# A graph network and mixture of experts on one core: attention's node blocks in thirteen pieces instead of ten

## Time and profile before

| | us |
|---|---|
| median of 3 runs | 1982.28 |
| lowest and highest | 1980.02, 2367.55 |
| the profiled execution | 1982.39 |
| its span, first to last instruction | 1980.4 |
| TensorE busy | 1654.1 (84%) |
| VectorE busy | 964.8 (49%) |
| GpSimd busy | 793.4 (40%) |
| ScalarE busy | 574.2 (29%) |
| mean granted clock of TensorE | 0.903 |

### The profile page before, as it was taken

How to read it: one execution, slowest core, us unless ns; L and a number is a source line. 1 busy time by engine, 2 the same in 40 slices (tenths; PEclk the granted TensorE clock), 3 DMA queues, 4 the chain that set the end, 5 groups by cost and what they waited for, 6 DMA issues and landing times.

```text
span 1980.4 us, 22491 instructions
## 1 busy us (share of the span) xinstructions
PE 1654.1 (84%) x6593; PEld 1039.0 (52%) x6593; DVE 964.8 (49%) x2223; ACT 574.2 (29%) x1334; POOL 793.4 (40%) x769
## 2 busy tenths in 40 slices
PE   5899575987979969997256889999899989989886
PEld 2454122444544545554133566667676766766665
DVE  5522141223333333434377677776676677764222
ACT  2121000212213223231022344343434344442321
POOL 1000565577656656000367545444445454420000
PEclk9899666998999989998667899999998999999888
DMA  7256454455445455201679755545545454421000
GB/s 244 112 181 217 132 137 134 114 158 147 129 143 160 130 172 133 85 17 59 190 226 281 227 146 151 148 138 159 151 132 159 141 167 139 143 84 33 19 6 8
DMA packets 191723, 269.97 MB, mean 136 GB/s; under 512 B 28484, under 2 KB 156193, under 8 KB 189025
## 3 DMA queue, kind: packets, MB, share of 16 engines
q1 hardware_dynamic: 147585, 144.74, 23.4%
q0 software_dynamic: 44000, 123.64, 22.5%
HBM read 196.22 MB, written 72.06 MB: 135 GB/s over the span
## 4 chain that ended last, share of the span: by engine, by line
PE 34%; DVE 6%; issue 4%; ACT 3%; SPq 1%; DMA 1%; POOL 1%; another core or an unknown queue 0%; POOLq 0%; ACTq 0%; DVEq 0%
PE att_psR L2262 8%; PE att_psR L2289 7%; PE att_psG L2147 5%; PE att_psR L2237 4%; PE att_psR L2246 4%; PE att_psQ L2123 1%; PE att_psR L2223 1%; PE att_psE L2130 1%; DVE att_stat L1911 1%; PE att_psR L2195 1%; POOL att_kv L1769 1%; PE att_psR L2200 1%; PE att_psR L2281 1%; DVE att_n L1922 1%; PE att_psG L2146 1%
## 5 line engine op out<-in xcount | busy, mean ns | idle before, releaser
L1769 POOL DMA_INDIRECT att_kv<-table_kv,g_srcI x314 | 357.9, 1140 | 502.7 <-PE att_psG L2147 274.5
L1085 POOL DMA_INDIRECT ex_hg<-table_h,z_idx x314 | 312.2, 994 | 185.5 <-issue 88.6
L1382 PE MATMUL ex_psG<-ex_hg,ex_oh 128*42 128x256 f32 x628 | 182.5, 433 | 59.0 <-issue 23.3
L2262 PE MATMUL att_psR<-att_t,g_mw 128*128 128x256 f32 x640 | 183.6, 438 | 18.6 <-ACT att_t L2101 18.6
L2147 PE MATMUL att_psG<-att_kv,att_oh 128*42 128x264 f32 x628 | 171.2, 414 | 1.8 <-issue 1.0
L2262 PEld LDWEIGHTS att_psR<-att_t,g_mw 128*128 128x128 f32 x640 | 135.7, 219 | 48.8 <-issue 28.2
L1382 PEld LDWEIGHTS ex_psG<-ex_hg,ex_oh 128*42 128x42 f32 x628 | 72.7, 130 | 168.8 <-issue 92.6
L1789 DVE TENSOR_TENSOR att_kv<-att_kv,att_epb 128x1024 f32<-128x1024 f32 x79 | 96.4, 1221 | 115.4 <-ACT att_epb L2058 97.2
L719 PE MATMUL tab_psH<-e_u,tab_xT 128*128 128x512 f32 x320 | 145.4, 607 | 7.2 <-DVE e_u L521 7.2
L2289 PE MATMUL att_psR<-g_mw,att_h 128*128 128x256 f32 x640 | 149.9, 382 | 0.0
L2289 PEld LDWEIGHTS att_psR<-g_mw,att_h 128*128 128x128 f32 x640 | 122.4, 192 | 20.4 <-issue 3.3
(11 more groups left out here) (308 smaller groups left out, 2443.4 us busy)
## 6 DMA issues: line engine op xcount, KB each, us to landing
table_h<-tab_hs SPq DMA_DIRECT2D x20, 1024.0 KB, 3.9
att_eft<-in_eft SPq DMA_DIRECT2D x158, 64.0 KB
ex_db<-table_dst SPq DMA_DIRECT2D x79, 126.0 KB
table_ohT<-ex_ohT SPq DMA_DIRECT2D x79, 126.0 KB
att_ohT<-table_ohT SPq DMA_DIRECT2D x79, 126.0 KB
table_oh<-ex_oh SPq DMA_DIRECT2D x79, 84.0 KB
att_oh<-table_oh SPq DMA_DIRECT2D x79, 84.0 KB
table_x<-e_x SPq DMA_DIRECT2D x10, 512.0 KB, 4.7
```

The costliest lines, as they stand in the source:

```text
L1085: nc.gpsimd.indirect_dma_start(hg[:, t % RING0, :], None, d.h[:, :], bass.IndirectOffsetOnAxis(ap=g.idx0[:, t:t + 1], axis=0)).then_inc(go ...
L1382: ins = nc.tensor.matmul(psG[0:WG, 0:D], oh[:, i % 3, t % TP, :], hg[:, t % RING0, :], start=(t % TP == 0), stop=last)
L1769: nc.gpsimd.indirect_dma_start(kv[:, t % (RINGC * TP), H:H + 2 * D], None, d.kv[:, :], bass.IndirectOffsetOnAxis(ap=g.srcI[:, t:t + 1], ax ...
L2262: ins = nc.tensor.matmul(out[:, c * CB:(c + 1) * CB], g.mw1[:, e, k, c * P:(c + 1) * P], t3[:, k, :], start=(k == 0), stop=(k == DK - 1))
```

## The change

`SEGMENTS` has thirteen pieces; `turnA` gets an own piece behind `att`, `turnN` and `turnX` too, and the first products `f` and `A` stand a slot behind their turn. `att` is now VectorE's part alone. In a slot where pieces of two blocks meet, `mix` stands behind `A` 2. The last block starts at slot 87 instead of 89. The banks: outside `f` to `norm` units turn over three; from the first `f` to `norm` they alternate on two (0 and 1) while `y` holds bank 2. The bursts of zero products are gone.

```diff
-WARM = 12
...
 SEGMENTS = (
     (("att", 0),),
+    (("turnA", 0),),
     (("wo", 0),),
-    (("turnN", 0), ("f", 0), ("f", 1), ("y", 0), ("f", 2), ("y", 1)),
-    (("f", 3), ("y", 2), ("f", 4), ("y", 3), ("f", 5), ("y", 4)),
-    (("f", 6), ("y", 5), ("f", 7), ("y", 6), ("y", 7), ("norm", 0)),
-    (("turnX", 0), ("A", 0), ("logits", 0), ("A", 1)),
-    (("mix", 0), ("A", 2), ("C", 0), ("A", 3)),
+    (("turnN", 0),),
+    (("f", 0), ("f", 1), ("y", 0), ("f", 2), ("y", 1), ("f", 3), ("y", 2)),
+    (("f", 4), ("y", 3), ("f", 5), ("y", 4), ("f", 6), ("y", 5)),
+    (("f", 7), ("y", 6), ("y", 7), ("norm", 0)),
+    (("turnX", 0),),
+    (("A", 0), ("logits", 0), ("A", 1)),
+    (("A", 2), ("mix", 0), ("C", 0), ("A", 3)),
     (("C", 1), ("A", 4), ("C", 2)),
     (("A", 5), ("C", 3), ("A", 6), ("C", 4)),
     (("A", 7), ("C", 5), ("C", 6), ("C", 7), ("out", 0)))
...
-    start = [(NG // NC + 1) * (b + 1) + LAG + 2 if slots else 8 * b + 1 for b in range(NC)]
+    start = [min((NG // NC + 1) * (b + 1) + LAG + 2, SLOTS + 1) if slots else 8 * b + 1 for b in range(NC)]
...
-        bank, before, last, turn_of = {}, {}, {}, 0
+        bank, before, last, turn_of, opened = {}, {}, {}, 0, False
         for what, b, e in order:
-            for unit in {"att": ("turnA",), "wo": ("wo",), ...
+            for unit in {"turnA": ("turnA",), "wo": ("wo",), ...
+                opened = opened or unit == "f"
                 if unit == "y":
                     n = 2
-                elif unit == "f":
-                    n = e % 2
+                elif opened:
+                    n = turn_of = (turn_of + 1) % 3 if turn_of == 2 else (turn_of + 1) % 2
                 else:
-                    n, turn_of = turn_of, (turn_of + 1) % 3
+                    n = turn_of = (turn_of + 1) % 3
...
+            opened = opened and what != "norm"
...
-                        if what == "att":
+                        if what == "turnA":
...
-                def warm(out):
...
-                        if what == "att":
+                        if what == "turnA":
                             out = take("turnA", b, e)
-                            warm(out)
                             pe.wait_ge(s.att_ready, b + 1)
...
                             out = take("turnN", b, e)
-                            warm(out)
...
                             out = take("turnX", b, e)
-                            warm(out)
```

More of the change, by code:

```diff
@@ L1713, in stage_attention @@
         assert redo or all(e > DONE_AFTER[b] for what, b, e in order if what == "load")
-        bank, before, last, turn_of = {}, {}, {}, 0
+        bank, before, last, turn_of, opened = {}, {}, {}, 0, False
         for what, b, e in order:
-            for unit in {"att": ("turnA",), "wo": ("wo",), "turnN": ("turnN",), "f": ("f",), "turnX": ("turnX",), "A": ("A",),
+            for unit in {"turnA": ("turnA",), "wo": ("wo",), "turnN": ("turnN",), "f": ("f",), "turnX": ("turnX",), "A": ("A",),
                          "logits": ("logits",), "mix": ("gateT", "bias"), "C": ("C",), "y": ("y",) if e == 0 else ()}.get(what, ()):
+                opened = opened or unit == "f"
                 if unit == "y":
                     n = 2
-                elif unit == "f":
-                    n = e % 2
+                elif opened:
+                    n = turn_of = (turn_of + 1) % 3 if turn_of == 2 else (turn_of + 1) % 2
                 else:
-                    n, turn_of = turn_of, (turn_of + 1) % 3
+                    n = turn_of = (turn_of + 1) % 3
                 bank[unit, b, e] = n
```

## The result

The changed kernel takes 1991.69 us (median of 19 runs, 1986.48 to 1998.76) against 1984.98 for the kernel before (19 runs): ratio 1.0027, 95% interval [1.0014, 1.0039]. Slower, by less than 2%. The forecast was 2010 us, +28, with a range of 1920 to 2042. Measured is +6.7 as the difference of the medians and +5.4 by the ratio, which is formed from the fast runs alone.

A forecast was written before the change was run, and what follows sets the result against it. TensorE was taken as the bound, starved in the new order by VectorE's chain. Period 88.9 + 6.5 of clock = 95.4 us; seven periods +35, slots 17 to 24 -14.5, slots 81 to 85 +11, end -3: +28, 2010 us, range 1920 to 2042.

The forecast's parts named there:

- a chain on VectorE from `norm` to the bias product: Place 6 to place 1: VectorE's then ScalarE's work sums to 33.6 us against TensorE's 21.6, so TensorE waits 12.0.
- place 7, scores' turn: TensorE waits about 3.7 us, as ScalarE's `root` of `norm` stands ahead of the scale this turn needs.
- two slots behind: In the two slots behind place 7's scores' turn, TensorE waits 2.2 us, part of the chain's 12.0.
- gates' copy: Around the gates, before the bias product at place 1, TensorE waits 6.1 us, part of the chain's 12.0.
- place 3, scores' turn: `wo` at place 2 delays place 3's turn: 2.9 us to the end of scale, less 0.8, a 2.2 us wait.
- place 5: ScalarE does exp, table load and gelu ahead of y4 there, a TensorE wait of 0.5 us.
- The clock: Half clock behind the gaps at places 3, 7 and 1 costs 6.5 us per block, bounds 1.7 and 13.
- The bank rule: `y` holds one bank, other units alternate on two until `norm`; it costs between zero and 0.5 us per block.
- Rival 1: Waits go and no new one comes; period 78 us, about 1880 us in all; chance 0.18.
- Rival 2: Half the chain hides: gates' stall stays, scores' turn and clock cost as now; period 86 to 90 us; chance 0.10.
- Rival 3: Clearly slower through the clock at places 7, 1 and 3, above 2022 us; chance 0.33.
- Rival 4: A bank holds a turn back, adding 0.5 us per block, 2014 us; chance 0.03.

The follow-up runs named there:

- e9: Changed kernel with three extra VectorE additions (1.95 us per block, results unused) at the logits of place 0, ahead of the gates; 1.0115 of the kernel before.
- e4: Changed kernel with ScalarE copying the turned gates ahead of the table load and gelu of A2; 0.9956 of the kernel before.
- e12: Changed kernel with ScalarE's scale ahead of roots, gates' copy ahead of A2's gelu, VectorE's subtract ahead of its add, `att` a slot later; 0.9772 of the kernel before.
- e10: Changed kernel with three extra VectorE additions (1.95 us per block, results unused) at `f` 5 in place 5; 1.0028 of the kernel before.
- e1: Changed kernel with the bursts of twelve zero products put back ahead of turnA, turnN and turnX; 1.0224 of the kernel before.
- e11: Changed kernel with its last block started at slot 89 as before, instead of 87; 1.0021 of the kernel before.
- e13: Changed kernel with the last block at slot 89 and the kernel before's bank rule for y; 1.0041 of the kernel before.
- e8: Changed kernel with blocks begun three slots later, ScalarE's scale ahead of the roots and gates' copy ahead of A2's gelu; 1.0069 of the kernel before.
- e5: Changed kernel with every block's start three slots later, the last at slot 90; 0.9953 of the kernel before.

## Why the prediction was right and wrong

**The mechanism held.** The period's gain was to be 8.2 us and was to be overdrawn by a chain on VectorE from `norm` to the bias product. Forecast for it 33.6 us, measured 32.3 to 32.5: in the block above from 1425.30, the carried row, to 1457.78, the bias product. e9 makes it longer, e4 and e12 shorter, and the period follows each time.

**The step that failed: the waits of a block, put at 14.7 us, are 10.8 in a full block.** By place:

| wait | forecast | the block above |
|---|---|---|
| place 7, scores' turn | 3.7 | 2.90 |
| two slots behind | 2.2 | 0.23, by a transfer |
| gates' copy | 6.1 | 5.30 |
| place 3, scores' turn | 2.2 | 2.35 |
| place 5 | 0.5 | none |

The first three are the chain's: 33.6 less 21.6 of TensorE's own work, 12.0, where 32.5 less 24.0, about 8.4, was measured. Three things make up the 3.6 between them, to rounding.

- 1.7 is counted twice. The prediction put 6.8 us of half clock behind place 7's gap, priced it at 1.4 instead of 3.4 since it "lies mostly under VectorE's chain", and added these 1.4 to the full wait of the chain. But TensorE's share of the chain was counted at full clock. The sums at half clock took 1.66 us more, and those came out of the wait, as e10's two blocks show.
- 1.1 is the chain, shorter than its terms. Half of it are the gates, taken at 5.8 from a block of before and 5.3 here. The 5.8 held 1.02 us of VectorE's wait for the exponential. Here its table was loaded at 1445.19, before its operand was there, and VectorE waited 0.28 us.
- 0.7 is work of TensorE beyond the 21.6.

**The clock** was forecast at 6.5 us per block. In a full block 92.3 - 10.8 - 75.9 leaves 5.6, where 75.9 is the work by the measured gaps of before (90.2 - 7.1 - 4.0 - 3.2 for 6.3 us of low clock). That is less than half of the 13.1 us at low clock, since some 2.5 of them lie in the gap ahead of the bias product, where there is nothing to slow. The forecast's 0.93 is what the row shows. Behind the gap of place 3 the clock held this time (sums 1.98 at 1481.19) and in e1 it did not (3.65), so a gap of 2.35 us can go either way.

The work stood in the sum as 74.2, 1.7 too low: the gaps of before were read from one block as 8.2 (7.1 on average), its clock as 3.6 (3.2), and 89.9 was the mean over full blocks and a lighter one. Together: work +1.7, waits -3.9, clock -0.9, that is -3.1 per full block, and seven of these are 22 us, the miss of the row. The 3.5 that the forecast took off for slots 79 and 80 are there: the last of the seven periods is 4.1 us shorter than the six before it. That the work was put too low hid 1.7 us of the miss in waits and clock; this much was luck.

The Trainium skill (TensorE: Matmul & The Clock Gate, "Loop structure matters more than you think") says that a copy by VectorE doesn't cool TensorE where the next products follow immediately. That condition isn't met here: TensorE stands idle for 2.90 and 5.30 us ahead of the rows at 1434.35 and 1457.78, and both gaps have half clock behind them. So the period of 88.9, which the prediction worked out for a clock that costs nothing, doesn't apply.
The Trainium skill (ScalarE: Activation LUTs, "What ACT_TABLE_LOAD costs") has 1.38 us of drain on top of a load. The rows above differ: the load of 1.28 at 1455.27 is followed by its gelu at 1456.57, with nothing between, and ScalarE's copy ahead of it ends at 1455.26.

**The other terms** were right within 1.6 us each: slots 17 to 24, slots 81 to 85, the end. That the end's -3 comes from the earlier start of block 9 is not shown, by e11. The bank rule was put at 0 to 0.5 us per block; e13 shows none beyond what two traces differ by.

**The rivals.** Rival 1 (waits go and none comes) fell with the waits' rows; its period of 78 is not reached by e12 either, at 85.2 in full blocks. Rival 2 (half of the chain hides) is refuted in its detail: both gaps stand, the clock costs more than before, and the period is above its 86 to 90. Rival 3 named places 7 and 1 rightly; it needed 8.1 us of clock per block, and 5.6 were lost. Rival 4 (a bank holds a turn back) isn't seen in e13.

## What to carry to other kernels

When a wait is removed by moving its product a step later, list for every slot what each in-order engine has in it, and look for slots where another engine now has more than the bound one. In such a stretch don't add the cost of a slow clock on the bound engine to its waits in full: in e10 3.1 us of it vanished in them. That holds only while no instruction of the late engine comes to wait for the slowed one: e1's burst of 2.51 us stood ahead of a turn that VectorE needed, and the chain grew by 2.5. So look at the hand-overs between the two, and how much room each has. What pays there is the order within the late engines: a copy ahead of a function that needs a table load, a subtract ahead of an add, a division a slot later gave 6.9 us per block together with no instruction removed. (The scale ahead of the square roots is part of it, with 2.4 us when run alone.)

## What was not expected of the hardware

Zero products meant to keep TensorE's clock up did the opposite in the new order: with three bursts per block back, the granted clock was 0.90 instead of 0.93 (19.5 us at half clock per block against 13.3), while in the old order their absence brought it from 0.96 to 0.94. In e8, with the waits of the scores' turn and the gates' copy shortened, it fell from e5's 0.94 to 0.90. The runs don't say why. They show that such a burst can help in one order and harm in another, so it has to be measured where it stands.
